# Early-fusion block on one core: the encoder's and the attention's middle turns written out, results placed directly in the output

## What is computed

```
for each of 4 layers (text tokens only):
    h = ln(h + softmax(q k^T / 4) v @ wo + bo)        # 12 heads of 16
    h = ln(h + relu(h @ w1 + b1) @ w2 + b2)           # 192 -> 768 -> 192
h = concat(image, text)                               # 8 x 561 x 192
h = h + attention(layernorm(h))                       # 12 heads of 64, own token masked
x = layernorm(h); probs = softmax(x @ gate_w); top 2 of 8 experts
h = h + sum over the 2 experts of prob * (gelu(x @ w_up + b_up) @ w_down + b_down)
```

## Time and profile before

| | us |
|---|---|
| median of 3 runs (lowest, highest) | 4164.06 (4157.66, 4174.01) |
| the profiled execution | 4161.31 |
| its span in the trace | 4159.6 |
| TensorE busy | 3763.3 (90% of the span) |
| VectorE, ScalarE, GpSimd busy | 2357.1, 2112.2, 1132.8 |
| mean granted clock of TensorE | 0.95 of full |

### The profile page before, as it was taken

One profiled execution on the slowest core, in us unless ns is written; L12 is line 12 of the kernel. 1 busy time (PEld: TensorE's weight loads), 2 busy tenths in 40 slices (PEclk: granted clock), 3 DMA queues, 4 the chain that ended last, 5 costly groups with the idle time before them and its releaser, 6 DMA issues. The chain is left out here.

```text
span 4159.6 us, 65381 instructions
## 1 busy us (share of the span) xinstructions
PE 3763.3 (90%) x21662; PEld 2485.8 (60%) x21662; DVE 2357.1 (57%) x4409; ACT 2112.2 (51%) x3234; POOL 1132.8 (27%) x1036
## 2 busy tenths in 40 slices
PE   4899999999999999999985899999999999939998
PEld 3355555555555555555543667666666666628887
DVE  6566666666666666666652546465564655634443
ACT  0555545455554545455541575675665756613332
POOL 5133323233332323323232010102111021034444
PEclk7899999999999999999987899999999999979999
DMA  7342333424333333423326111111111111115664
GB/s 172 96 119 85 102 106 89 117 75 119 92 105 90 96 111 84 126 75 111 96 79 212 42 28 34 37 32 39 35 32 36 32 39 34 26 74 140 149 141 108
DMA packets 237691, 355.05 MB, mean 85 GB/s; under 512 B 40208, under 2 KB 138528, under 8 KB 234000
## 3 DMA queue, kind: packets, MB, share of 16 engines
q1 hardware_dynamic: 213344, 294.23, 24.9%
q0 software_dynamic: 23376, 57.40, 6.2%
q10 hardware_dynamic: 768, 0.79, 0.1%
HBM read 225.70 MB, written 112.63 MB: 81 GB/s over the span
## 5 line engine op out<-in xcount | busy, mean ns | idle before, releaser
L643 DVE TENSOR_REDUCE mx<-ring 128x2 f32<-128x1024 f32 x768 | 919.6, 1222 | 502.1 <-PE ring L406 498.2
L535 ACT ACTIVATE probs<-ring 128x1024 f32<-128x1024 f32 x768 | 767.7, 1025 | 413.9 <-PE ring L419 412.8
L1734 DVE TENSOR_REDUCE a_nmx<-a_ring 128x1 f32<-128x561 f32 (+1 forms) x480 | 344.3, 736 | 198.1 <-PE a_ring L1392 102.1
L1453 ACT ACTIVATE a_ring<-a_ring,a_nmx 128x561 f32<-128x561 f32 (+1 forms) x480 | 334.0, 696 | 216.9 <-DVE a_nmx L1734 215.6
L406 PE MATMUL ring<-k_stack,q_stack 48*128 48x512 f32 x1536 | 359.9, 481 | 63.4 <-ACT probs L535 22.9
L419 PE MATMUL ring<-q_stack,k_stack 64*128 64x512 f32 x1536 | 362.7, 489 | 53.3 <-DVE mx L643 39.7
L1292 POOL TENSOR_SCALAR_AFFINE_SELECT a_probs<-a_probs 128x256 f32<-128x256 f32 (+1 forms) x240 | 95.4, 397 | 1131.2 <-ACT a_probs L1489 1085.3
L433 PE MATMUL acc<-probs,vals 128*32 128x512 f32 x3072 | 396.6, 637 | 1.3 <-ACT probs L535 1.3
L1489 ACT ACTIVATE a_probs<-a_ring 128x561 f32<-128x561 f32 (+1 forms) x480 | 287.5, 637 | 175.1 <-PE a_ring L1392 172.2
L1392 PE MATMUL a_ring<-a_k_hh,a_q_hl 128*128 128x256 f32 (+1 forms) x960 | 312.3, 340 | 23.6 <-DVE a_q_hl L1714 11.4
L419 PEld LDWEIGHTS ring<-q_stack,k_stack 64*128 64x128 f32 x1536 | 142.6, 189 | 287.6 <-DVE mx L643 101.4
(11 more groups left out here) (231 smaller groups left out, 6916.7 us busy)
## 6 DMA issues: line engine op xcount, KB each, us to landing
q_stack<-qk_scratch SPq DMA_DIRECT2D x576, 64.0 KB, 2.3
k_stack<-qk_scratch SPq DMA_DIRECT2D x576, 64.0 KB, 2.4
qk_scratch<-qk_hi SPq DMA_DIRECT2D x32, 768.0 KB, 3.6
qk_scratch<-qk_lo SPq DMA_DIRECT2D x32, 768.0 KB, 5.1
a_q_hm<-a_q_hl SPq DMA_DIRECT2D x48, 280.5 KB
a_k_hh<-a_k_hh SPq DMA_DIRECT2D x48, 280.5 KB
tokens<-h_out SPq DMA_DIRECT2D x33, 384.0 KB, 2.7
h_in<-tokens SPq DMA_DIRECT2D x32, 384.0 KB, 4.0
```

The source lines that it names most:

```text
L535: nc.scalar.activation(probs[n % 2][:, pair:pair + 2, x // 2, :], buf[:, :, :], ACT.Exp, scale=DK ** -0.5).then_inc(act, 1)
L643: nc.vector.tensor_reduce(mx[s][:, i, :].rearrange("p (r t) -> p r t", r=2)[:, :, t], buf[:, :, :], AX, ALU.max).then_inc(dve, 1)
L1453: nc.scalar.activation(buf, buf, ACT.Exp, bias=nmx[0:r, i, h:h + 1], accum_out=sums[0:r, i, h:h + 1]).then_inc(act, 1)
L1734: nc.vector.tensor_reduce(nmx[0:r, i, h:h + 1], flat(buf)[0:r, 0:N], AX, ALU.max, negate=True).then_inc(dve, 1)
```

## The change

1. The loops of 13 turns in the encoder and of 5 turns in the attention become Python loops, on every engine: each turn is written out, and each value that a turn waits for is a constant.
2. The internal array `fused` is gone: the name now stands for the output itself. Attention stores its rows there, and the experts' indirect DMAs add to them there. The output has no rows beyond 4488, so these DMAs are given a bound, `B * N - 1`, and told to leave out rows past it. The zeroing of the 512 extra rows and the final copy with its wait are removed.

```diff
-            with pe.Fori(0, LOOPS) as it:
+            for it in range(LOOPS):
                 steps(R_LOOP, it)
...
-            sp.dma_start(fused[B * N:B * N + BLOCK, :].rearrange("(p i) d -> p i d", i=4), empty[:, :, 0:D]).then_inc(filled, 16)
...
-            sp.wait_ge(filled, 16 * (NBLOCKS + 1))
+            sp.wait_ge(filled, 16 * NBLOCKS)
...
             for s in (0, 1):
                 sp.wait_ge(scattered[s], 64 * ((NBLOCKS + 1 - s) // 2))
-            flat = lambda t: t.rearrange("r d -> (r d)").rearrange("(p f) -> p f", p=P)
-            sp.dma_start(flat(out_dram[0:B * N, :]), flat(fused[0:B * N, :])).then_inc(stored, 16)
-            sp.wait_ge(stored, 16)
...
                         g.indirect_dma_start(fused, bass.IndirectOffsetOnAxis(ap=ids[:, n, i:i + 1], axis=0),
-                                             y[n % 2][:, i, :], None, compute_op=ALU.add).then_inc(scattered[n % 2], 16)
+                                             y[n % 2][:, i, :], None, bounds_check=B * N - 1, oob_is_err=False,
+                                             compute_op=ALU.add).then_inc(scattered[n % 2], 16)
...
-    fused = internal("fused", [B * N + BLOCK, D])
+    fused = out.rearrange("b n d -> (b n) d")
```

More of the change, by code:

```diff
@@ L243, with encoder_phase @@
     closes = staticmethod(last_part)
-def encoder_phase(nc, dram, tokens, table, slots_in, fused):
+def encoder_phase(nc, dram, tokens, table, slots_in):
     TURNS = LAYERS * B // 2
@@ L548, in _ @@
                 steps(R, 0)
-            with sc.Fori(0, LOOPS) as it:
+            for it in range(LOOPS):
                 steps(R_LOOP, it)
@@ L691, in _ @@
                 steps(R, 0)
-            with v.Fori(0, LOOPS) as it:
+            for it in range(LOOPS):
                 steps(R_LOOP, it)
@@ L784, in _ @@
                 steps(R, 0)
-            with g.Fori(0, LOOPS) as it:
+            for it in range(LOOPS):
                 steps(R_LOOP, it)
@@ L960, in _ @@
                 steps(R, 0)
-            with sp.Fori(0, LOOPS) as it:
+            for it in range(LOOPS):
                 steps(R_LOOP, it)
@@ L1810, in added, with blocks_phase @@
         return {"mm": {"t": 1, "up": 1, "down": 1}, "act": {"up": 1, "hi": 1}, "dve": {"t": 2, "down": 2, "lo": 1}}[name].get(step[0], 0)
-def blocks_phase(nc, dram, table_dram, slots_in, fused, which, mine, out_dram):
+def blocks_phase(nc, dram, table_dram, slots_in, fused, which, mine):
     R = Region(Blocks, [], blocks_steps(), {n: 0 for n in Blocks.names}, 0, range(BUFFERS))
@@ L1835, in blocks_phase @@
         ring = [ctx.enter_context(nc.psum_tensor(f"m_ring{i}", [P, 512], F32)) for i in range(BUFFERS)]
-        fixed_in, mm, act, dve, shared, stored = (sem(n) for n in ("fixed_in", "mm", "act", "dve", "shared", "stored"))
+        fixed_in, mm, act, dve, shared = (sem(n) for n in ("fixed_in", "mm", "act", "dve", "shared"))
         scattered = [sem(f"scattered{k}") for k in range(2)]
@@ L1962, in build @@
     tokens = internal("tokens", [(B + 1) * N, D])
-    fused = internal("fused", [B * N + BLOCK, D])
+    fused = out.rearrange("b n d -> (b n) d")
     table = internal("expert_table", [EXPERTS * P, ROW])
     slots_in = internal("slots_in", [NBLOCKS * BLOCK, XW])
-    encoder_phase(nc, dram, tokens, table, slots_in, fused)
+    encoder_phase(nc, dram, tokens, table, slots_in)
     with ExitStack() as ctx:
@@ L1970, in build @@
         attention_phase(nc, dram, tokens, fused, slots_in, which, mine)
-        blocks_phase(nc, dram, table, slots_in, fused, which, mine, out.rearrange("b n d -> (b n) d"))
+        blocks_phase(nc, dram, table, slots_in, fused, which, mine)
 def kernel(**inputs):
```

## The result

The changed kernel takes 4138.15 us (median of 5 runs, 4134.83 to 4145.09) against 4167.96 for the kernel before, run beside it: ratio of the two 0.9933, 95% interval 0.9917 to 0.9949. That is 28 to 30 us less. Forecast were 4112 and 4082 to 4132: the sign is as forecast, the time is 26 us above the forecast and 6 above the range. The profiled execution took 4137.14 us, its span is 4135.0, so the two spans differ by 24.6 us.

The account below looks back on a forecast made before the run. TensorE was taken as the bound, busy 3763 of 4160 us. From 4161.3: register work -4, encoder clock -13, attention -23, end -10, bound on adds +0.5, giving 4112 us, range 4082 to 4132.

Parts of the forecast that it names:

- Encoder, register work: Encoder loop turns: register instructions and branch gone, 0.3 us in each of 13 turns, 4 us less.
- what is left on the path is the rest of the difference: Encoder: register work on the path costs 3.9 - 3.7 = 0.2 us a turn, taken as 0.3.
- Encoder, clock: Encoder turns: clock falls remain in some three quarters of half turns, 1 us a turn saved, 13 us in all.
- Rival 2: Encoder: the clock falls stay in every turn, 0 instead of 13 us gained, 4125 us; chance 0.17.
- 48 us for all falls: Encoder: upper bound if every clock fall is saved, 13 x 3.7 = 48 us.
- Attention: Attention: four taken branches of 6.0 us and 1.5 us of register work go, less 2 us: 23 us gone.
- the 2 us I had allowed: Attention: 2 us taken off the gain for a clock fall that may come elsewhere in one of five turns.
- The end: Kernel's end: copy and its wait go, GpSimd's drain after the last add ends last, 10 us gone.
- Bound, code, zeroing: Bound on the experts' last two adds costs 0.5 us (0 to 1.2); fetching written-out code and removing the zeroing: nothing.
- rival 3: Encoder: TensorE waits for code, 6.0 us in each of 13 turns, 78 us slower, 4190 us; chance 0.04.
- Rival 1: Encoder: the clock stays at 1.00 in its turns, 48 instead of 13 us gained, 4077 us; chance 0.16.

Follow-up runs that it names:

- e1: The kernel before with only the encoder's loop written out on its five engines: 4165.09 us, ratio 0.9997.
- e8: The changed kernel with the encoder's loops put back and four more repeated score-product pairs per half turn before the two waits for VectorE's maxima: 4082.09 us, ratio 0.9784.
- e7: The changed kernel with four more repeated score-product pairs per encoder half turn, before the two waits for VectorE's maxima: 4087.72 us, ratio 0.9804.
- e14: The changed kernel with the encoder's loops back, e7's repeated pairs and one extra product before the wait for GpSimd's layer norm: 4084.06 us, ratio 0.9801.
- e5: The changed kernel with one pair of score products issued twice per encoder half turn, in a stretch without idle time: 4138.16 us, ratio 0.9914.
- e16: The changed kernel with e7's repeated pairs, one extra product before the wait for GpSimd's layer norm, and e5's doubled pair: 4088.01 us, ratio 0.9813.
- e12: The kernel before with only attention's five middle turns written out: 4146.8 us, ratio 0.9952.
- e2: The changed kernel with the encoder's loops put back, so attention written out and results straight to the output: 4131.6 us, ratio 0.9922.
- e9: The kernel before, all loops kept, with e7's repeated score-product pairs alone: 4116.55 us, ratio 0.9881.
- e6: The kernel before, loops kept, with only the adds made straight into the output with a bound, copy and zeroing gone: 4156.65 us, ratio 0.9971.

## Why the prediction was wrong

**Encoder, register work (4 us forecast): nothing.** The failed step is "what is left on the path is the rest of the difference". The 0.2 us were the remainder of 3.9 less 3.7, and the 3.7 was not exact: half of the first half's 2.3 us is 1.15, not 1.4, and by the `hT` markers of half turns in the kernel before the falls cost 2.4 and 1.5 us (67.15 for 64.79, 65.93 for 64.45). That is all of the 3.9, and nothing is left for register work. e1 measured -1 us (-5 to +3). e8 against e7 shows no cost at full clock either; only where the waits are filled as well (e14) do 0.2 us a turn come out.

**Encoder, clock (13 us forecast): nothing, and 4 us worse in the profiled runs.** This was the step that carried the miss. I reasoned that a turn that lost its register work would meet the chip's decision at other moments and so lose some falls. But the register work had not been on TensorE's path, so nothing moved there; and had it been, e5 against e16 speaks for a settled turn with falls staying in step with them through changes of 0.46 us. The falls come 133.12 us apart in the kernel before, in the changed one and in e5 from 661.33 us on. Where moments did shift, in e1, some half turns lost their fall and others grew, and the mean stayed at 132.94 us. Rival 2, to which I gave 0.17, came true. What I held against it, that the period was that of a turn with register work, is the part that was wrong.

Under that step lies a reading that misled: I took the clean second turn and the slow loop turn as written-out code against a loop. e12 has the encoder's code of before and no clean second turn, e2 has one again. By these traces it was chance, and no property of written-out code. Nor were there two such turns in a row, as the prediction has it: the turn ahead of it, 112.92 to 230.40 us, stands at 0.95, with falls at other places. Of 4.3 us that the encoder's last marker is later, 3.95 are this one turn (133.19 for 129.24).

The size of 48 us for all falls was right: e7 takes 50 us off the changed kernel, e9 49 off the one before.

The Trainium skill, "TensorE: Matmul & The Clock Gate", section "A second HAM failure mode: psum-queue depth-cycling", says that frequent very short idle times between groups of products are enough to make the clock go back and forth. This case agrees: the longest wait ahead of the encoder's falls is 0.85 us, and with it and the next one filled all but three falls from 500 us to the end of the middle turns go (e7).

**Attention (23 us forecast): 19.8.** The branches' price was right: turns of 168.1, and e12 alone measured 19 to 20. Two places took more than the 2 us I had allowed. One is in the turn from 3084.70, 3.3 us at 0.98, after a wait of 1.3 us for VectorE (L1713). The other is behind the last turn, where the stretch to the experts' first gather grew from 119.5 to 121.84 us and TensorE is busy 2.2 us longer with the same work; the changed kernel has a fall more there, at 0.50 from 3651.9 to 3655.3 us. Windows of that stretch, before and changed:

```profile
3610.20:3729.70 119.50, 65.23 (x441) 46.28 (x440) 51.46 (x216) 36.32 (x72) 30.49 (x42) 0.80 0.06 20
```

```profile
3592.40:3714.24 121.84, 67.41 (x443) 48.48 (x443) 52.12 (x217) 36.94 (x74) 30.42 (x42) 0.80 0.06 20
```

In this term the allowance for falls elsewhere was the mis-sized part: some 5.6 us in the traces, not 2.

**The end (10 us forecast): 10.8 from the last add on; e6 measured 12 (6 to 18).** Right, and by the mechanism named: GpSimd's drain of 2.58 us is last.

**Bound, code, zeroing.** The bound costs nothing (forecast 0.5, bounds 0 to 1.2). The code queue moved 0.9 MB more and no turn of the encoder from the second on took over 133.31 us (133.18 in the loop), so rival 3 is out. Rival 1 was out for this change, yet it is what e7 makes of the kernel.

The sum again with what the two traces show: rival 2 gave 4124.8. Add 4 for register work that was hidden, 4.3 for the encoder's early turn, 3.2 for attention, 1.2 for the experts' phase (1.7 measured, 0.5 forecast for the bound), less 0.8 at the end: 4136.7, and 4137.14 was measured.

## What to carry to other kernels

Before a slow turn is blamed on its code, look at the same turn in more than one trace. Where every turn has its falls at the same place and the same length, small savings and small costs may vanish in them: here 0.46 us a turn did in settled turns with falls, and 0.38 of it came back without them. Idle time of TensorE well under a microsecond can cost more than itself; filling it by issuing products again into the buffers that they hold anyway was worth 49 us here, and removing the encoder's loop 1 (-3 to +5). A loop on TensorE is to be judged by its branch's row: 0.2 us left nothing to gain, 3.65 us with the idle time and the slow stretch behind it gave 20 in four turns.

## What the runs showed of the hardware

- In the settled turns the falls recur every 133.12 us in three kernels whose turns differ by register work or by 0.46 us of products; in a fourth (e1) the turns vary from 131.97 to 134.88. How much work a turn in step with them can take up before it lets go was not tried.
- Dose: one further pair before the 0.85 us wait leaves the falls in nearly all turns (4133.53 us), three and one more leave three falls from 500 us to the end of the middle turns (4087.72), and with two products ahead of the transposes as well none is left there (4087.46).
- An indirect DMA that adds in memory takes 1554 ns to issue with a bound, into the output, and 1575 without one, into an internal array (medians; 1574 to 1575 in the four traces without a bound, 1554 to 1556 in the fourteen with one). Which of the two differences does it was not tried.
- Why one fall in attention comes in just one of its turns (in nearly every kernel without the loop there, at about the same turn) was not tried.
